# Rounding the head of h on VectorE, and fetching the scan's x operands two steps ahead

## The chip, the cores and the metric

The kernel runs on one core of a Trainium2 chip. The metric is device microseconds of one execution. The kernel before took 646.58, 649.59 and 651.04 us in three runs, median 649.59 us. The profile of it is of one further execution, of 646.94 us, whose span (first to last instruction) is 644.9 us.

## The reference, cut to what matters

Two layers. The first (fc1, a nearest-neighbour graph in 8x8 windows, an edge convolution with a maximum over neighbours, fc2, a residual) ends in an image x1 of 16 x 48 x 32 x 32. The second scans the rows of x1 with a ConvLSTM cell, once from the top and once from the bottom, and projects the hidden states of both:

```
def step(carry, xr):
    h, c = carry
    inp = jnp.concatenate([xr, h], axis=1)
    gates = lax.conv_general_dilated(inp, w_mid, (1,), 'SAME', dimension_numbers=dn) + b[None, :, None]
    i, f, g, o = jnp.split(gates, 4, axis=1)
    c2 = jax.nn.sigmoid(f) * c + jax.nn.sigmoid(i) * jnp.tanh(g)
    h2 = jax.nn.sigmoid(o) * jnp.tanh(c2)
    return ((h2, c2), h2)
hs_f = _convlstm_scan(xr, w_f[:, :, 1, :], b_f, reverse=False)
hs_b = _convlstm_scan(xr, w_b[:, :, 1, :], b_b, reverse=True)
feats = jnp.concatenate([hs_f, hs_b], axis=2)
feats = jnp.transpose(feats, (1, 2, 0, 3))
y = jnp.einsum('oc,bchw->bohw', w_proj, feats)
...
return jax.nn.relu(y) + x
```

## The kernel before, in words

The first layer is worked in 32 groups, called turns here; TensorE gathers neighbours with one-hot matmuls, ScalarE applies the GELU (`gel`), VectorE takes maxima (`hmax`, L1272), finds the next groups' neighbours (`idx`, L1248) and builds the one-hot operand (`onehot`, L1257). The neighbour indices go out to memory and come back spread over partitions: SP, whose queue issues nearly every transfer, stores `idx` (L326), waits until it has landed, and issues two spreads into `ib` (L335). Each turn SP also loads `xres` (L319), keys (L309) and `y_hl` (L300) and stores x1 rows (L345). The rows of x1 are split on the way into a rounded head and a rest and lie in `xh`, one slot a row. In turns 14 to 21 SP adds to each turn the weights of the scan (`wl_raw`, L404), small columns (`rests`, L420), a store of two finished rows to memory (`xl_d`, `store_lows`, L414) and a copy of two rows' twins within on-chip memory (`load_twins`, L426); rows 16 to 23 follow in turns 26 to 29 and rows 8 to 15 in scan steps 2 to 5.

The scan has 32 steps s of two directions d. For each, TensorE adds into two banks (`pz` or `p_edge`) an x part from `xt` (2 matmuls, L728), a top part from `xh` with the head of h (6 matmuls, L738), and a low part from `ht` (6 matmuls, L746: the rest of h, an unrounded copy of h, and a third of x). ScalarE takes tanh of the two banks (L926, L932), copies the other direction's h into `ht` (`h_edge`, L942), and takes tanh of the cell (L936). VectorE computes `cu` (L1370), `pz` (L1378), `c` (L1381) and `h` (L1388), in program order: cell of direction 0, `cu` of direction 1, cell of direction 1, `cu` of direction 0 of the next step. GpSimd (POOL) then rounds h into the slot of the next row in `xh` (`head`, L1155) and subtracts that head from h into `ht` (L1157). Each engine runs its own program in order; semaphores tie them. VectorE's steps 2 to 13 are a hardware loop, the others are written out.

SP in a scan step, for each direction: wait for the gates of this step, load the thirds of the next step into `ht` (a single buffer, L439), load the shifted x two steps ahead into `xt` (two buffers, L432), store h (`hist_d`, L493), load a residual row (`x1r`). From step 17 on it then loads two stored rows of h into `hp` (L503), after both directions. TensorE projects them (L757) one step later, between the x part and the top part of direction 0; from step 19 on ScalarE copies the projected row out (L947) and VectorE takes its statistics (`bst`, L1393).

Of the kernel before, what the change touches and what calls it, by code (L numbers as in the profile page):

```python
# [54 lines left out]
def build(nc, xs, xrow, w1, ones_sel, col1, jcol, wedge, edge_scale, edge_shift, ident9, w2, col2,  # L55
# [9 lines left out]
    with ExitStack() as ctx:  # L65
# [193 lines left out]
        @block.sync
        def _(sp):  # L260
# [180 lines left out]

            def turn(j, b):
                if isinstance(j, int) and nth(j, b, 0)[0] in (GROUPS - 4, GROUPS - 3):
# [3 lines left out]
                    sp.wait_ge(S["xl_stored0"], 32 * 8)  # L447
                    load_shifts(0, d)
                    load_thirds(0, d)
                    load_shifts(1, d)  # L450
# [4 lines left out]
                if isinstance(j, int) and j > 0:  # L455
                    at = nth(j, b, 0)[0] - (GROUPS - 18)
                    if at == 0:
                        sp.wait_ge(S["rests_set"], 1)
# [1058 lines left out]
```

## Time and profile before

| | us |
|---|---|
| median of 3 runs (lowest, highest) | 649.59 (646.58, 651.04) |
| the profiled execution, its span | 646.94, 644.9 |
| PE, DVE, ACT, POOL busy (share of span) | 549.8 (85%), 500.1 (78%), 437.1 (68%), 242.5 (38%) |
| first layer: first to last `hmax` | 76.1 to 348.8 |
| scan: first h to last h | 352.7 to 622.9 |

The busy shares are means over stages with different limits. In the first layer VectorE has work nearly all the time; in the scan no engine has, since each direction is a loop of dependent work and two such loops share the engines. An idle gap counts only where the work that ends last stands behind it.

### The profile page before, as it was taken

Reading aid. Unit: us, or ns where it says so; the run is one execution under the profiler, and the core shown is the slowest. Engines: PE = TensorE matmul, PEld = TensorE weight load, DVE = VectorE, ACT = ScalarE, POOL = GpSimd, SP = SyncE. Lnnn points to the kernel's source line nnn. Section 1 sums busy time; section 2 is a strip of 40 time slices with the busy share of each in tenths; the row PEclk is TensorE's granted clock in tenths of the full one; section 3 lists DMA queues with packets and bytes.
Section 4 is the critical chain, followed back from the end, with each engine's and each line's share of the span. In section 5 each row is a group of like instructions: output and inputs, shape, how many; then the busy total and the mean of one; then the engine's idle time right before and its main releaser. Section 6 shows DMA issues by size and latency. Waiting matters only on the chain.

```text
span 644.9 us, 11504 instructions
## 1 busy us (share of the span) xinstructions
PE 549.8 (85%) x3160; PEld 333.0 (52%) x3160; DVE 500.1 (78%) x963; ACT 437.1 (68%) x645; POOL 242.5 (38%) x299
## 2 busy tenths in 40 slices
PE   6983699999999978989868989999997988998860
PEld 1232466666665645656535555566664645555530
DVE  2587679999999998799988757777777466776765
ACT  4761379999999978689866655666665455565645
POOL 2740103333333332235834634444444233443310
PEclk9995589999999999799997999999999898999985
DMA  8847656656667877878653355444444444444416
GB/s 220 271 143 220 168 132 134 148 144 142 142 142 163 196 168 182 176 153 161 159 129 77 87 137 143 127 134 130 130 127 137 116 148 129 132 128 121 131 55 196
DMA packets 112517, 94.72 MB, mean 147 GB/s; under 512 B 54560, under 2 KB 86818, under 8 KB 112146
## 3 DMA queue, kind: packets, MB, share of 16 engines
q1 hardware_dynamic: 111714, 90.64, 55.3%
q10 hardware_dynamic: 768, 3.67, 2.2%
q8 instruction: 15, 0.25, 0.2%
q14 instruction: 20, 0.16, 0.1%
HBM read 65.61 MB, written 26.48 MB: 143 GB/s over the span
## 4 chain that ended last, share of the span: by engine, by line
DVE 31%; PE 19%; DMA 15%; issue 12%; SPq 12%; ACT 7%; POOL 2%; DVEq 1%; POOLq 0%; ACTq 0%
DVE hmax L1272 8%; DMA hp<-hist_d 5%; PE pz L738 4%; DVE onehot L1257 4%; DVE c L1381 3%; DVE cu L1370 3%; DMA idx_d<-idx 3%; PE pz L580 3%; DVE idx L1248 3%; PE p_edge L738 2%; DVE h L1388 2%; PE pz L746 2%; DMA x_d<-x1t 2%; SPq L426 2%; DVE pz L1378 2%
## 5 line engine op out<-in xcount | busy, mean ns | idle before, releaser
L1272 DVE TENSOR_REDUCE hmax<-gel 96x128 f32<-96x1024 f32 x128 | 151.9, 1204 | 11.0 <-ACT gel L871 10.9
L871 ACT ACTIVATE gel<-pz 96x1024 f32<-96x1024 f32 x128 | 130.5, 1020 | 31.7 <-PE pz L658 18.2
L1155 POOL CAST xh<-h 48x512 fp32r<-48x512 f32 x62 | 37.6, 606 | 145.3 <-DVE h L1388 143.1
L738 PE MATMUL pz<-xh,w_rows 128*112 128x512 f32 x258 | 72.2, 416 | 5.9 <-POOL xh L1155 5.7
L1157 POOL TENSOR_TENSOR ht<-h,xh 48x512 fp32r<-48x512 f32 x62 | 73.6, 1186 | 5.0
L746 PE MATMUL pz<-ht,w_rows 128*112 128x512 f32 x258 | 69.3, 404 | 3.7 <-DMA ht<-xl_d 3.7
L658 PE MATMUL pz<-onehot,ab_hi 64*96 64x512 f32 x256 | 60.4, 468 | 5.2 <-ACT gel L871 3.9
L738 PEld LDWEIGHTS pz<-xh,w_rows 128*112 128x112 f32 x258 | 43.2, 178 | 35.3 <-POOL xh L1155 17.3
L936 ACT ACTIVATE pz<-c 48x512 f32<-48x512 f32 x43 | 25.7, 599 | 50.2 <-DVE c L1381 50.2
L746 PEld LDWEIGHTS pz<-ht,w_rows 128*112 128x112 f32 x258 | 44.8, 177 | 22.6 <-DMA ht<-xl_d 7.6
L1257 DVE TENSOR_SCALAR onehot<-ib,jcol_sb 128x1024 fp32r<-128x1024 uint16 x64 | 48.1, 753 | 10.3 <-DMA ib<-idx_d 10.2
L1388 DVE SCALAR_TENSOR_TENSOR h<-tgo,pz 48x512 f32<-48x512 f32 x43 | 29.7, 690 | 30.6 <-ACT pz L936 29.4
L658 PE MATMUL pz<-ident,ab_lo 64*96 64x512 f32 x256 | 53.0, 408 | 0.0
L658 PE MATMUL pz<-ident,ab_hi 64*96 64x512 f32 x256 | 52.9, 407 | 0.0
L658 PE MATMUL pz<-onehot,ab_lo 64*96 64x512 f32 x256 | 52.8, 408 | 0.0
L1108 POOL TENSOR_TENSOR xh<-x1t,x1c 48x256 f32 (+1 forms) x32 | 32.4, 1012 | 49.4 <-DVE onehot L1257 48.8
L1094 POOL TENSOR_TENSOR x1t<-side,xres 112x256 f32<-112x256 f32 x32 | 24.1, 752 | 62.3 <-ACT side L878 42.4
L1370 DVE SCALAR_TENSOR_TENSOR cu<-pz,c 48x512 f32<-48x512 f32 x43 | 29.9, 695 | 18.3 <-ACT pz L926 17.5
L606 PE MATMUL p_keys<-kr,kl 128*64 128x64 f32 x512 | 23.2, 236 | 22.1 <-DVE idx L1248 11.1
L942 ACT ACTIVATE ht<-h 48x512 fp32r<-48x512 f32 x62 | 39.2, 632 | 1.5
L658 PEld LDWEIGHTS pz<-onehot,ab_hi 64*96 64x96 f32 x256 | 21.4, 162 | 33.1 <-issue 22.9
L738 PE MATMUL p_edge<-xh,w_rows 128*112 128x512 f32 x126 | 36.2, 424 | 2.3 <-POOL xh L1155 2.0
(147 smaller groups left out, 1136.3 us busy)
## 6 DMA issues: line engine op xcount, KB each, us to landing
ib<-idx_d SPq DMA_DIRECT2D x64, 256.0 KB, 4.4
xt<-xl_d SPq DMA_DIRECT2D x64, 197.6 KB
y_d<-y SPq DMA_DIRECT2D x32, 192.0 KB, 3.3
y_hl<-y_d SPq DMA_DIRECT2D x32, 192.0 KB, 4.0
hist_d<-h SPq DMA_DIRECT2D x62, 96.0 KB, 4.8
hp<-hist_d SPq DMA_DIRECT2D x30, 192.0 KB, 3.3
ht<-xl_d SPq DMA_DIRECT2D x128, 33.1 KB, 2.9
xl_d<-xh SPq DMA_DIRECT2D x16, 198.4 KB, 3.4
```

The lines of the kernel that those rows point to most:

```text
L658: mm = pe.matmul(pz[0:O, 2 * (t % 2) + s, :], part[rows, b, t, which], moving[rows], start=(n == 0), stop=(n == 3))
L738: pe.matmul(gate_banks(k, d)[m][0:TOP, :], w_rows[:, 0, d, m, t], by_column(row), start=False, stop=False)
L746: mm = pe.matmul(gate_banks(k, d)[m][0:TOP, :], w_rows[:, 1, d, m, t], by_column(ht[:, d, t:t + (W + 1) * B]), start=False, stop=(t == TAP ...
L871: act.activation(gel[:, t % 2], pz[0:O, 2 * (t % 2):2 * (t % 2) + 2, :], ACT.Gelu) \
L942: act.activation(h_slots(ht, HALF, d), h2[0:C, d].rearrange("p (b w) -> p b w", w=W), ACT.Copy) \
L1108: pool.tensor_tensor(slots(0, g)[:, 0], by_row(x1t[0:C, b]), by_row(x1c[0:C]).bitcast(F32), ALU.subtract).then_inc(S["x1_half"], 1)
L1155: pool.tensor_copy(head, columns(h2[0:C, d])).then_inc(S["h_top"], 1)
L1157: pool.tensor_tensor(h_slots(ht, 0, d), columns(h2[0:C, d]), head.bitcast(F32), ALU.subtract).then_inc(S["h_lo"], 1)
L1257: dve.tensor_scalar(onehot[:, b, 2 * half:2 * half + 2], ib[:, b, 2 * half:2 * half + 2], jcol_sb[:, 0:1], None, ALU.is_equal).then_inc(S[ ...
L1272: dve.tensor_reduce(dst, gel[:, t % 2].rearrange("p w (r c k) -> p w r c k", r=WS, k=KN), AX_X, ALU.max).then_inc(S["maxed"], 1)
L1370: dve.scalar_tensor_tensor(cu[HALF:TOP, d], gate_banks(k, d)[0][HALF:TOP, :], 1.0, c2[HALF:TOP, d], ALU.add, ALU.mult).then_inc(S["cells_k ...
L1388: dve.scalar_tensor_tensor(h2[0:C, d], tgo[HALF:TOP, d], 1.0, b_go[HALF:TOP, :], ALU.add, ALU.mult) \
```

## The change

1. VectorE rounds h into `xh` itself, right behind `h`, and with that takes over POOL's waits for the row stores. POOL only subtracts. VectorE's loop over steps 2 to 13 is written out.
2. `ht` has two buffers for each direction; the thirds are loaded two steps ahead, in the same place of SP's order.
3. The load of stored h moves from the end of SP's step to the middle, behind the store of direction 0.
4. Row stores and twin copies take four rows instead of two, and lie in turns 10, 11 and 18, 19 and 26, 27 (stores), 12, 13 and 20, 21 and 30, 31 (twins), and scan steps 2 and 3; weights go in turns 8 to 20, `rests` in 21 to 25. SP's program is written out from turn 8 on (from 14 before).

```diff
-        ht = sb("ht", [P, 2, SLOT], F32R)
+        ht = sb("ht", [P, 2, 2, SLOT], F32R)
...
-                sp.dma_start(xl_d[r:r + 2, first:first + rows].rearrange("r c n -> c r n"),
-                             xh[src:src + rows, r:r + 2, 0:SLOT - 1].bitcast(F32)).then_inc(S[sem], 16)
+                sp.dma_start(xl_d[r:r + 4, first:first + rows].rearrange("r c n -> c r n"),
+                             xh[src:src + rows, r:r + 4, 0:SLOT - 1].bitcast(F32)).then_inc(S[sem], 16)
...
-                    if at < 8:
-                        block, part = divmod(at, 4)
-                        sp.wait_ge(S["x1_split"], PAIRS * (block + 1))
-                        store_lows((0, 24)[block] + 2 * part, "xl_stored0")
-                        load_twins((0, 24)[block] + 2 * part, "x_twins0")
...
+                    if 8 <= g < 16:
+                        load_scan_weight(g - 8)
+                    elif 16 <= g < 21:
+                        load_tap_weight(g - 16)
+                    elif 21 <= g < 26:
+                        load_rest(g - 21)
+                    for first, r, n in ((10, 0, 0), (18, 24, 0), (26, 16, 1)):
+                        if first <= g < first + 2:
+                            sp.wait_ge(S["x1_split"], first - 2)
+                            store_lows(r + 4 * (g - first), f"xl_stored{n}")
+                        elif g in (first + 2, first + 3) and n == 0 or g >= 30 and n == 1:
+                            load_twins(r + 4 * (g % 2), f"x_twins{n}")
...
             def step(s):
                 for d in range(2):
-                    if s + 1 < H:
+                    if s + 2 < H:
                         sp.wait_ge(S["gates"], s * 4 + (2 * d + 2))
-                        load_thirds(s + 1, d)
-                    if s + 2 < H:
+                        load_thirds(s + 2, d)
                         load_shifts(s + 2, d)
                     store_h(s, d)
+                    if s >= H // 2 + 1 and d == 0:
+                        load_h(s - 1, 1 - s % 2)
                     if 6 <= s < H // 2 + 6:
                         load_x1r(s - 6, d)
-                    if 2 <= s < 6:
-                        (store_lows, load_twins)[d](4 + 2 * s, ("xl_stored1", "x_twins1")[d])
-                if s >= H // 2 + 1:
-                    load_h(s - 1, 1 - s % 2)
+                    if 2 <= s < 4:
+                        (store_lows, load_twins)[d](4 * s, ("xl_stored1", "x_twins1")[d])
...
-                pool.wait_ge(S["h2_ready"], s * 2 + (d + 1))
...
-                pool.tensor_copy(head, columns(h2[0:C, d])).then_inc(S["h_top"], 1)
                 pool.wait_ge(S["h_top"], s * 2 + (d + 1))
...
                 dve.scalar_tensor_tensor(h2[0:C, d], tgo[HALF:TOP, d], 1.0, b_go[HALF:TOP, :], ALU.add, ALU.mult) \
                     .then_inc(S["h2_ready"], 1)
+                if s + 1 < H:
+                    if s == 0:
+                        dve.wait_ge(S["xl_stored0"], 32 * 4)
+                    if s == 7 and d == 0:
+                        dve.wait_ge(S["xl_stored1"], 32 * 4)
+                    if s == H // 2 - 1 and d == 0:
+                        dve.wait_ge(S["gates"], 4 * (s + 1))
+                    dve.wait_ge(S["h2_ready"], s * 2 + (d + 1))
+                    dve.tensor_copy(head_slots(s + 1, d), h2[0:C, d].rearrange("p (b w) -> p b w", w=W)) \
+                        .then_inc(S["h_top"], 1)
...
-            with dve.Fori(0, 2) as j:
-                for k in range(2, 8):
-                    step(j * 6 + k, k)
-            for s in range(14, H):
+            for s in range(2, H):
```

VectorE in one scan step, from `c` of direction 0 on. Before:

```order
L1381 SCALAR_TENSOR_TENSOR c<-cu,pz 48x512 [waits cell_parts]
L1388 SCALAR_TENSOR_TENSOR h<-tgo,pz 48x512 [waits h_edge,h_lo,hist0,tanh_c]
L1370 SCALAR_TENSOR_TENSOR cu<-p_edge,c 48x512 [waits cells,tanh_if]
L1378 SCALAR_TENSOR_TENSOR p_edge<-p_edge,tgo 48x512 [waits cells_kept,tanh_go]
L1381 SCALAR_TENSOR_TENSOR c<-cu,p_edge 48x512 [waits cell_parts]
L1388 SCALAR_TENSOR_TENSOR h<-tgo,p_edge 48x512 [waits h_edge,h_lo,hist1,tanh_c]
```

Now:

```order
L1371 SCALAR_TENSOR_TENSOR c<-cu,pz 48x512 [waits cell_parts]
L1378 SCALAR_TENSOR_TENSOR h<-tgo,pz 48x512 [waits h_edge,h_lo,hist0,tanh_c]
L1388 CAST xh<-h 48x16x32 [waits h2_ready]
L1360 SCALAR_TENSOR_TENSOR cu<-pz,c 48x512 [waits cells,tanh_if]
L1368 SCALAR_TENSOR_TENSOR pz<-pz,tgo 48x512 [waits cells_kept,tanh_go]
L1371 SCALAR_TENSOR_TENSOR c<-cu,pz 48x512 [waits cell_parts]
L1378 SCALAR_TENSOR_TENSOR h<-tgo,pz 48x512 [waits h_edge,h_lo,hist1,tanh_c]
L1388 CAST xh<-h 48x16x32 [waits h2_ready]
```

One CAST stands between each `h` and the next `cu`, twice in a step; nothing else of VectorE's order in a step is changed (line numbers are those of each kernel's own text).

SP in a turn of the first layer, from the `ib` spreads to the next store of `idx`. Before (turns 14 to 18 have all four kinds of added transfers, 19 to 21 those without `rests`):

```order
L335 DMA ib<-idx_d 64x4x512 [waits onehots,idx_stored0]
L335 DMA ib<-idx_d 64x4x512
L404 DMA wl_raw<-wl 16x1344
L420 DMA rests<-ones_sel 16x1
L414 DMA xl_d<-xh 48x2x529 [waits x1_split]
L414 DMA xl_d<-xh 16x2x529
L426 DMA xh<-xh 16x2x529 x2
L319 DMA xres<-xrow 48x256 [waits x1_sum]
L319 DMA xres<-xrow 48x256
L326 DMA idx_d<-idx 128x4x8 [waits topk_done]
```

Now, the turns with the most (12 and 13):

```order
L339 DMA ib<-idx_d 64x4x512 [waits onehots,idx_stored1]
L339 DMA ib<-idx_d 64x4x512
L408 DMA wl_raw<-wl 48x1344
L430 DMA xh<-xh 16x4x529 x2
L323 DMA xres<-xrow 48x256 [waits x1_sum]
L323 DMA xres<-xrow 48x256
L330 DMA idx_d<-idx 128x4x8 [waits topk_done]
```

The store of rows is in other turns; the twin copies are one issue pair of twice the rows.

SP in a scan step after the 17th (`hist_d<-h` is the store of h, `ht<-xl_d` the thirds), from the store of direction 0 on. Before:

```order
L493 DMA hist_d<-h 48x512 [waits h2_ready]
L517 DMA x1r<-x_d 64x512
L439 DMA ht<-xl_d 16x529 [waits gates]
L439 DMA ht<-xl_d 16x529
L432 DMA xt<-xl_d 96x1x527
L493 DMA hist_d<-h 48x512 [waits h2_ready]
L511 DMA x1r<-x_d 48x512
L503 DMA hp<-hist_d 96x512 [waits hist0,hist1]
L503 DMA hp<-hist_d 96x512
```

Now:

```order
L492 DMA hist_d<-h 48x512 [waits h2_ready]
L502 DMA hp<-hist_d 96x512 [waits hist0,hist1]
L502 DMA hp<-hist_d 96x512
L516 DMA x1r<-x_d 64x512
L443 DMA ht<-xl_d 16x529 [waits gates]
L443 DMA ht<-xl_d 16x529
L436 DMA xt<-xl_d 96x1x527
L492 DMA hist_d<-h 48x512 [waits h2_ready]
L510 DMA x1r<-x_d 48x512
```

The load of `hp` stands in front of direction 1's thirds, shifts and store of h, instead of behind them.

## Rows read from the trace of the kernel before

**Rows 1.** VectorE in time (start us, us, what): `hmax` that ends a turn

```profile
214.27 0.69 DVE L1264 TENSOR_TENSOR hmax<-hmax,selfg 96x512 f32<-96x512 f32 x1
...
222.22 0.69 DVE L1264 TENSOR_TENSOR hmax<-hmax,selfg 96x512 f32<-96x512 f32 x1
...
295.58 0.69 DVE L1264 TENSOR_TENSOR hmax<-hmax,selfg 96x512 f32<-96x512 f32 x1
```

**Rows 2.** The same view, in brackets the idle time before: a late `ib`

```profile
333.17 0.75 DVE L1257 TENSOR_SCALAR onehot<-ib,jcol_sb 128x1024 fp32r<-128x1024 uint16 x1 [1.70 <-DMA ib<-idx_d]
```

**Rows 3.** SP's queue in time, an undisturbed turn

```profile
159.80 1.45 SPq L335 DMA_DIRECT2D ib<-idx_d  x2
...
162.11 0.85 SPq L319 DMA_DIRECT2D xres<-xrow  x2
...
164.35 0.43 SPq L326 DMA_DIRECT2D idx_d<-idx  x1
```

**Rows 4.** The same view, what a loaded turn adds: weights, row store, twins

```profile
248.35 0.60 SPq L404 DMA_DIRECT2D wl_raw<-wl  x1
...
249.00 0.90 SPq L414 DMA_DIRECT2D xl_d<-xh  x2
...
249.94 1.44 SPq L426 DMA_DIRECT2D xh<-xh  x2
```

**Rows 5.** VectorE in time, written-out scan: h, cu, next h

```profile
463.73 0.69 DVE L1388 SCALAR_TENSOR_TENSOR h<-tgo,pz 48x512 f32<-48x512 f32 x1 [0.67 <-ACT pz L936]
...
464.45 0.69 DVE L1370 SCALAR_TENSOR_TENSOR cu<-p_edge,c 48x512 f32<-48x512 f32 x1
...
467.34 0.69 DVE L1388 SCALAR_TENSOR_TENSOR h<-tgo,p_edge 48x512 f32<-48x512 f32 x1 [0.67 <-ACT p_edge L936]
```

**Rows 6.** VectorE in time, one-time work for the projection, step 17

```profile
483.81 1.12 DVE L1414 TENSOR_SCALAR wp_sb<-wp_sb 96x64 f32<-96x64 f32 x1
```

**Rows 7.** VectorE in time, hardware loop: h, direction 0, consecutive steps

```profile
448.70 0.69 DVE L1388 SCALAR_TENSOR_TENSOR h<-tgo,pz 48x512 f32<-48x512 f32 x1 [0.86 <-ACT pz L936]
...
456.31 0.69 DVE L1388 SCALAR_TENSOR_TENSOR h<-tgo,p_edge 48x512 f32<-48x512 f32 x1 [0.86 <-ACT p_edge L936]
```

**Rows 8.** Casts: VectorE's by source (ns min/median/max), POOL's on the page

```profile
L1195 DVE CAST y<-x_in x9: 427/489/647, 7.4 to 28.4; 128x512 fp32r<-128x512 f32 x9
...
L1155 POOL CAST xh<-h 48x512 fp32r<-48x512 f32 x62 | 37.6, 606 | 145.3 <-DVE h L1388 143.1
```

**Rows 9.** TensorE in time: two top parts in a row without a wait

```profile
520.86 1.67 PE L738 MATMUL pz<-xh,w_rows 128*112 128x512 f32 x6
...
524.26 1.59 PE L738 MATMUL pz<-xh,w_rows 128*112 128x512 f32 x6
```

**Rows 10.** VectorE in time: h of direction 0 in steps 0, 18 and 31

```profile
352.68 0.69 DVE L1388 SCALAR_TENSOR_TENSOR h<-tgo,pz 48x512 f32<-48x512 f32 x1 [0.66 <-ACT pz L936]
...
494.71 0.69 DVE L1388 SCALAR_TENSOR_TENSOR h<-tgo,pz 48x512 f32<-48x512 f32 x1 [0.66 <-ACT pz L936]
...
618.07 0.69 DVE L1388 SCALAR_TENSOR_TENSOR h<-tgo,p_edge 48x512 f32<-48x512 f32 x1 [0.66 <-ACT p_edge L936]
```

**Rows 11.** TensorE by lines, scan (busy, mean ns; idle before)

```profile
L746 PE MATMUL pz<-ht,w_rows 128*112 128x512 f32 x252 | 67.7, 404 | 3.7 <-DMA ht<-xl_d 3.7
...
L757 PE MATMUL p_keys<-hp,wp_sb 96*64 96x512 f32 x32 | 9.5, 676 | 10.3 <-DMA hp<-hist_d 10.3
```

**Rows 12.** VectorE in time with projection: h, cu, next step's h

```profile
547.66 0.69 DVE L1388 SCALAR_TENSOR_TENSOR h<-tgo,pz 48x512 f32<-48x512 f32 x1 [0.67 <-ACT pz L936]
...
548.88 0.69 DVE L1370 SCALAR_TENSOR_TENSOR cu<-p_edge,c 48x512 f32<-48x512 f32 x1 [0.53 <-ACT p_edge L926]
...
556.03 0.69 DVE L1388 SCALAR_TENSOR_TENSOR h<-tgo,pz 48x512 f32<-48x512 f32 x1 [0.67 <-ACT pz L936]
```

**Rows 13.** Busy us in 4 us (PE, PEld, DVE, ACT, POOL), PEclk, DMA

```profile
500.00:504.00 4.00, 4.00 (x12) 2.27 (x9) 0.00 (x0) 0.00 (x0) 0.93 (x1) 0.50 0.57 178
```

**Rows 14.** Transfers to or from `hist_d` in the scan

```profile
DMA to landing us min/median/max: 1.9/4.6/7.2
```

More of the change, by code:

```diff
@@ L249, in by_row, with h_slots, head_slots @@
             return t.rearrange("c (r w) -> c r w", w=W)
-        def h_slots(t, first, d):
-            return t[first:first + C, d, 1:1 + (W + 1) * B].rearrange("p (b w) -> p b w", w=W + 1)[:, :, 0:W]
+        def h_slots(first, d, b):
+            return ht[first:first + C, d, b, 1:1 + (W + 1) * B].rearrange("p (b w) -> p b w", w=W + 1)[:, :, 0:W]
         def row_of(s, d):
             return s if d == 0 else s * -1 + (H - 1)
+        def head_slots(s, d):
+            return xh[0:C, row_of(s, d), 1:1 + (W + 1) * B].rearrange("p (b w) -> p b w", w=W + 1)[:, :, 0:W]
         @block.sync
@@ L425, in load_twins @@
                 for first, src in ((C, HALF), (TOP, HALF + 16)):
-                    sp.dma_start(xh[first:first + 16, r:r + 2, 0:SLOT - 1].bitcast(F32),
-                                 xh[src:src + 16, r:r + 2, 0:SLOT - 1].bitcast(F32)).then_inc(S[sem], 16)
+                    sp.dma_start(xh[first:first + 16, r:r + 4, 0:SLOT - 1].bitcast(F32),
+                                 xh[src:src + 16, r:r + 4, 0:SLOT - 1].bitcast(F32)).then_inc(S[sem], 16)
             def load_shifts(s, d):
@@ L438, in load_thirds @@
                 for q in range(2):
-                    sp.dma_start(ht[HALF * q + C:HALF * q + HALF, d, 0:SLOT - 1].bitcast(F32),
-                                 xl_d[row_of(s, d), 32 + 16 * q:C + 16 * q]).then_inc(S[f"x_third{d}"], 16)
+                    sp.dma_start(ht[HALF * q + C:HALF * q + HALF, d, s % 2, 0:SLOT - 1].bitcast(F32),
+                                 xl_d[row_of(s, d), 32 + 16 * q:C + 16 * q]).then_inc(S[f"x_third{d}{s % 2}"], 16)
             def turn(j, b):
@@ L446, in turn @@
                     sp.wait_ge(S["pads_set"], 8)
[L447 to L450, printed above, removed]
+                    sp.wait_ge(S["xl_stored0"], 32 * 4)
+                    for s in range(2):
+                        load_shifts(s, d)
+                        load_thirds(s, d)
                 for k, stage in ((0, load_xres), (3, store_idx), (-2, store_x1), (5, load_keys), (4, load_y),
@@ L480, in _ @@
                 turn(0, b)
-            with sp.Fori(1, GROUPS // 2 - 9) as j:
+            with sp.Fori(1, 4) as j:
                 for b in range(2):
                     turn(j, b)
-            for j in range(GROUPS // 2 - 9, GROUPS // 2):
+            for j in range(4, GROUPS // 2):
                 for b in range(2):
@@ L540, in _ @@
                 step(s)
-            sp.wait_ge(S["xl_stored1"], 32 * 8)
+            sp.wait_ge(S["xl_stored1"], 32 * 4)
             for b in range(2):
@@ L739, in h_part @@
                                   start=False, stop=False)
-                pe.wait_ge(S[f"x_third{d}"], s * 32 + 32)
+                pe.wait_ge(S[f"x_third{d}{s % 2}"], s // 2 * 32 + 32)
                 if later(s):
@@ L774, in _ @@
             pe.wait_ge(S["first_rows"], 2)
-            pe.wait_ge(S["x_twins0"], 32 * 8)
+            pe.wait_ge(S["x_twins0"], 32 * 4)
             pe.wait_ge(S["wl_split"], 3)
@@ L787, in _ @@
                 step(s, s)
-            pe.wait_ge(S["x_twins1"], 32 * 8)
+            pe.wait_ge(S["x_twins1"], 32 * 4)
             for s in range(8, 14):
@@ L937, in tanh_cell, with h_edge @@
                     .then_inc(S["tanh_c"], 1)
-            def h_edge(s, d):
+            def h_edge(s, d, b):
                 act.wait_ge(S["h2_ready"], s * 2 + (d + 1))
-                act.activation(h_slots(ht, HALF, d), h2[0:C, d].rearrange("p (b w) -> p b w", w=W), ACT.Copy) \
+                act.activation(h_slots(HALF, d, b), h2[0:C, d].rearrange("p (b w) -> p b w", w=W), ACT.Copy) \
                     .then_inc(S["h_edge"], 1)
@@ L950, in step @@
                 for d in range(2):
[L951 removed]
+                    prev = (s - 1, 1, k % 2) if d == 0 else (s, 0, (k + 1) % 2)
                     more = later(s) if d == 0 else not isinstance(s, int) or s + 1 < H
@@ L1080, in first_rows @@
             def first_rows():
-                pool.wait_ge(S["xl_stored0"], 32 * 8)
+                pool.wait_ge(S["xl_stored0"], 32 * 4)
                 for n, row in enumerate((0, H - 1)):
@@ L1148, in columns @@
                     return t.rearrange("p (b w) -> p b w", w=W)
-                pool.wait_ge(S["h2_ready"], s * 2 + (d + 1))
-                if s == H // 2 - 1 and d == 0:
-                    pool.wait_ge(S["gates"], 4 * (s + 1))
-                head = xh[0:C, reg(row_of(s + 1, d), 0, 1), 1:1 + (W + 1) * B] \
-                    .rearrange("p o (b w) -> p (o b) w", w=W + 1)[:, :, 0:W]
-                pool.tensor_copy(head, columns(h2[0:C, d])).then_inc(S["h_top"], 1)
                 pool.wait_ge(S["h_top"], s * 2 + (d + 1))
-                pool.tensor_tensor(h_slots(ht, 0, d), columns(h2[0:C, d]), head.bitcast(F32),
+                pool.tensor_tensor(h_slots(0, d, (s + 1) % 2), columns(h2[0:C, d]), head_slots(s + 1, d).bitcast(F32),
                                    ALU.subtract).then_inc(S["h_lo"], 1)
```

23 lines of the change are left out of this document (4 added, 19 removed).

## The prediction, made before the changed kernel was run

> **What bounds the kernel now.** I read the chain of waits first, to see which engine is named in which stretch, then each engine's instructions in time in the three stretches that the change touches, then TensorE's groups with the idle time in front of them. In the first layer VectorE should be the bound: an undisturbed turn takes 222.22 - 214.27 = 7.95 us [rows 1]. The next eight turns, to 295.58, take 73.36 us where 8 x 7.95 = 63.6 would do, so 9.8 us are lost there; they are the turns whose `onehot` waits for a late `ib`, as it does once more at the end of the layer, for 1.70 us [rows 2]. What is late is SP. In an undisturbed turn SP has issued `ib` by 161.25 and can store the next `idx` at 164.35; of these 3.10 us `xres` takes 0.85, so 2.25 are free [rows 3]. A loaded turn adds 0.60 for weights, 0.90 for a row store and 1.44 for twins, 2.94 in all [rows 4]. SP falls back by 0.7 us or more a turn, and the `idx` store that it issues too late delays everything behind it.
>
> In the scan two loops of dependent work share the engines. TensorE needs 524.26 - 520.86 = 3.40 us for one direction's half-step, when nothing holds it [rows 9]. VectorE in the written-out steps needs 467.34 - 463.73 = 3.61 from h to h [rows 5]: `cu`, `pz`, `c`, 0.67 waiting for the tanh of the cell, h. Two halves are 7.22. In VectorE's hardware loop a step takes 456.31 - 448.70 = 7.61 [rows 7], since there h starts 0.86 rather than 0.67 behind the work before it. From step 0 to 18 the scan takes 494.71 - 352.68 = 142.0 us, 7.89 a step; from 18 to 31, with projection, 618.07 - 494.71 = 123.4 us, 9.49 a step [rows 10]. TensorE's idle time says what the difference to the smooth step is: 3.7 us before the low part, waiting for `ht`, and 10.3 us before half of the projections, waiting for `hp` [rows 11]. A step with projection that does not wait takes 556.03 - 547.66 = 8.37 [rows 12].
>
> **The change, part by part.** The sum is made against the profiled execution, 646.94 us; the median of the runs, 649.59, is 2.65 higher.
>
> *First layer.* The heaviest new turn has weights and the twins of four rows. If a copy of four rows costs SP what one of two rows did, that is 0.60 + 1.44 = 2.04, under the 2.25 that are free [rows 3, 4]; if it costs twice, 3.48, and SP falls back 1.2 us in each of two turns, twice, with unloaded turns behind them. The turns with row stores add 1.50. Gain at most 9.8, at least nothing (if `idx` lands as late as before); I take 8.0, since even the bad case loses in four turns rather than eight. At the end of the layer turns 28 and 29 lose their rows and twins and get two pairs of thirds: of the 1.70 [rows 2] I take 1.5. Together -9.5.
>
> *Scan, steps 0 to 18.* POOL's rounding (0.606) leaves the way from h to TensorE and a cast on VectorE comes in. The nearest row is VectorE's cast of 512 words, 0.427 at its shortest, 0.489 median, 0.647 at most, undisturbed at the low end [rows 8]. Its output there is contiguous; here it goes into 16 runs of 32 words, which no VectorE row shows. I take 0.43, with 0.03 to the next instruction as between h and `cu` (464.45 - 463.73 = 0.72 for an h of 0.69 [rows 5]): 0.46. TensorE gets the head about 0.2 us earlier, but VectorE works in order: `cu` of the other direction, and through it that direction's next h, now stand behind the cast. Half a step on VectorE becomes 3.61 + 0.46 = 4.07, a step 8.14. That is above TensorE's 6.80 and above the 7.61 of today, so VectorE alone sets the pace, and what waits for `ht` there was (3.7) or hardware loop (0.4 a step) is covered by it. 18 x 8.14 = 146.5, plus 1.1 of one-time work [rows 6], is 147.6 against 142.0: +5.6. This part costs time.
>
> *Scan, steps 18 to 31.* Projection adds VectorE's statistics and ScalarE's copy. In the unstalled step `cu` of direction 1 stands idle 0.53 behind ScalarE [rows 12]; the cast behind h of direction 0 fits into that. The other cast adds 0.46: 8.37 + 0.46 = 8.83, and 13 x 8.83 = 114.8 against 123.4, -8.6, if no projection waits. SP issues the load half a step, some 4 us, earlier, and TensorE's longest total here was 10.3 us over the projections of one bank. In front of the load SP now waits for h of the previous step to be stored: a transfer to or from `hist_d` takes 4.6 us at the median and 7.2 at most [rows 14], against about 4.4 between the two events, so SP is usually held little and at most some 2.8; behind it stand direction 1's thirds and shifts, due two steps later, and its store of h, due 4 us later. I take -8.0.
>
> *Doubled `ht`, four-row transfers in steps 2 and 3, the subtraction that starts earlier:* no price of their own, since TensorE's slack of 4.07 - 3.40 = 0.67 a half-step covers them; without it the 3.7 us of waits for `ht` [rows 11] would be what they can cost or give. *The tail* behind the last h is as before.
>
> Sum: 646.94 - 9.5 + 5.6 - 8.0 = 635.0.
>
> **Weighed against the Trainium skill.** The trace has the cast of 512 words at 0.427 us or more [rows 8]. The Trainium skill (VectorE: DVE Perf Modes, the section on the TRN2 errata) gives 58 cycles plus the elements over the mode's factor at 0.96 GHz: (58 + 256)/0.96, an estimate of 0.33 us. By the row the sum is 635.0; by the page each cast is 0.10 shorter, and the sum would be about 630. The row decides.
>
> **The rivals.**
>
> *The cast runs at one word a cycle, because of its runs of 32* (12 in 100). Nothing in the profile shows a fast VectorE write into such runs. Its price would be that of VectorE's other 512-word work, 0.69 [rows 5]: 0.26 more in 36 halves up to step 18 (9.5 us), in 13 halves of direction 1 (3.4), and 0.2 in direction 0's, where 0.53 was free (2.6): 650.5, slower than before. The gain is gone when the cast takes about 0.62, and beyond 0.73 the kernel is slower by over 1%. Against it speaks only that its source is one contiguous run. The same page of the Trainium skill (the section on what auto-detection checks) would have a single-source copy between SBUF tensors keep its doubled rate if the outer dimensions are even, which 16 is; no row of this case shows it.
>
> *SP stays late in the first layer* (13 in 100): four-row twins cost twice, and `idx` lands behind larger transfers. Then the 8.0 is missing: 643.0. Against it: only four turns carry twins, not eight.
>
> *`hp` stays late* (10 in 100): held by the wait for the stored h, the load starts no earlier than now, and each step with projection keeps 9.49 and gets the 0.46: 13 x 9.95 = 129.4, +6.0 in place of -8.0, 649.0.
>
> *TensorE's clock falls in the scan* (5 in 100). Behind one wait for `hp` the granted clock was 0.50, that is 1.2 GHz, from 500 to 504 us, with VectorE idle in all of it [rows 13]. TensorE will idle 16% of a step (6.80 of 8.14). At half the clock its half-step is 6.8, a step 13.6 and 5.5 too long: two such steps eat the gain, four make it slower by 1%; six, 668. Against it: the drop stood behind a long wait, and what idles now is 0.67 at a time.
>
> **How the numbers follow.** The forecast, with VectorE as the scan's bound and SP on time, gets 60 in 100 and gives 635; since the profiled execution is the low end of three runs that spread 0.7%, I say 636 for the median. About 1% is what a measurement here can tell from no change. Best case: 9.8 and 1.7 in the first layer, 8.6 in the scan: 632.4, less the 3.0 by which the lowest run lies under its median: 629. The upper end takes in late SP and late `hp` and reaches 650, at the edge of the slow cast. Faster by over 1% means under 643.1: the forecast's 60, half of late SP (7), and 1 of late `hp`: 0.68. Slower by over 1%, above 656.1: 5 of the slow cast and 3 of the clock, 0.08. The rest, 0.24, within 1%.
>
> **What would show it.** Right: `hmax` rows 7.95 apart from 222 to 296 with no `onehot` behind `ib`; a cast of 0.43 between each h and `cu`; h of one direction 8.1 apart up to step 18 and 8.8 after it, with `cu` no longer idle behind ScalarE; no wait for `ht` and next to none for `hp`; no PEclk at 0.5 in the scan. Wrong: a cast near 0.7; steps still at 7.6, which would mean that VectorE is not held; `ib` waits in the turns with twins; `hp` waits of over 1 us.

## The result, and the profile after

Over 20 runs each the changed kernel takes 642.07 us at the median, the kernel before 646.91; the ratio is 0.9933, 95% interval 0.9905 to 0.996. (The ratio is not quite that of the medians, since it leaves out the few runs that fell into a slower state.) It is faster by 0.7%, where 2% was forecast. The profiled execution took 645.08 us, 3.0 above its median, with a span of 643.3 us.

VectorE in time (start us, us, line, operation, idle time before in brackets and what ended it) answers to [rows 1]. Up to the first row shown the turns are 7.95 us apart, as forecast, the last of them 8.25; then come two bad ones, of 9.60 and 11.97 us:

```profile
198.81 0.69 DVE L1254 TENSOR_TENSOR hmax<-hmax,selfg 96x512 f32<-96x512 f32 x1
...
202.19 0.75 DVE L1247 TENSOR_SCALAR onehot<-ib,jcol_sb 128x1024 fp32r<-128x1024 uint16 x1 [1.56 <-DMA ib<-idx_d]
...
208.41 1.08 DVE L1254 TENSOR_TENSOR hmax<-hmax,selfg 96x512 f32<-96x512 f32 x1
...
220.38 0.69 DVE L1254 TENSOR_TENSOR hmax<-hmax,selfg 96x512 f32<-96x512 f32 x1
...
332.54 0.75 DVE L1247 TENSOR_SCALAR onehot<-ib,jcol_sb 128x1024 fp32r<-128x1024 uint16 x1 [3.28 <-DMA ib<-idx_d]
```

Two more turns, to 277.31 and 286.15, take 9.18 and 8.84. Over turns 1 to 25 that is 8.2 us above 7.95 a turn; the kernel before lost 10.2 by the same count. The last row answers to [rows 2]: the wait at the layer's end is 3.28 us, not gone, as forecast, but twice as long.

SP's queue in time, behind rows 4 to 7's store and ahead of the bad turns, answers to [rows 3, 4]:

```profile
181.15 2.83 SPq L323 DMA_DIRECT2D xres<-xrow  x2
...
188.82 1.34 SPq L430 DMA_DIRECT2D xh<-xh  x2
190.21 1.31 SPq L323 DMA_DIRECT2D xres<-xrow  x2
191.56 0.43 SPq L330 DMA_DIRECT2D idx_d<-idx  x1
...
196.94 1.33 SPq L339 DMA_DIRECT2D ib<-idx_d  x2
```

The copy of four rows' twins costs SP 1.34 us, no more than that of two (1.44). Two things are late. Behind a four-row store the issue of `xres` takes 2.83 us in place of 0.85 (3.34 a turn before), so SP itself falls back. And the landing is late: `idx` was stored at 191.56, and SP, which waits for it, could issue `ib` only at 196.94. The windows of the same stretch (busy us of PE, PEld, DVE, ACT, POOL; PEclk; share of the DMA engines; GB/s) show how much the DMA engines carry then:

```profile
190.00:198.00 8.00, 6.94 (x54) 4.33 (x50) 7.69 (x20) 7.07 (x11) 1.30 (x3) 1.00 0.99 174
198.00:206.00 8.00, 7.54 (x66) 4.88 (x66) 6.33 (x19) 6.57 (x10) 2.72 (x4) 1.00 0.95 143
206.00:214.00 8.00, 5.68 (x40) 4.28 (x42) 6.56 (x11) 4.75 (x7) 2.52 (x4) 0.75 0.96 186
```

The DMA engines are 95 to 99% busy; in undisturbed turns, from 110 to 142 us, the share is 0.60 to 0.62. The share is no exact measure: a short window can come out above 1 (1.28 below). And the clock falls: TensorE's keys come late (first row below), it does nothing from 206 to 208 us, and from 210 to 216 its granted clock is half, 1.2 GHz (second row). In the turn of 11.97 no `onehot` waits for `ib`; the late keys and the half clock make it. The layer's end has the same: 0.50 from 334 to 342 us, behind the 3.28 us wait.

```profile
208.32 0.69 PE L604 MATMUL p_keys<-kr,kl 128*64 128x64 f32 x16 [2.58 <-DMA kr<-xn_d]
```

```profile
212.00:214.00 2.00, 2.00 (x10) 1.83 (x12) 2.00 (x6) 1.83 (x3) 0.73 (x1) 0.50 1.28 150
```

This is not new in the change. In the kernel before, in the turn of 11.60 us within the 73.36 of [rows 1], the keys come 1.71 us late and the granted clock is 0.50 from 260 to 266 us:

```profile
258.32 0.69 PE L606 MATMUL p_keys<-kr,kl 128*64 128x64 f32 x16 [1.71 <-DMA kr<-xn_d]
```

```profile
262.00:264.00 2.00, 2.00 (x12) 1.83 (x10) 1.33 (x6) 1.87 (x3) 0.11 (x1) 0.50 0.99 219
```

In the scan the steady rhythm is the one forecast. VectorE from h to h, to be held against [rows 5]:

```profile
455.45 0.69 DVE L1378 SCALAR_TENSOR_TENSOR h<-tgo,pz 48x512 f32<-48x512 f32 x1 [0.66 <-ACT pz L934]
456.17 0.42 DVE L1388 CAST xh<-h 48x512 fp32r<-48x512 f32 x1
456.62 0.69 DVE L1360 SCALAR_TENSOR_TENSOR cu<-p_edge,c 48x512 f32<-48x512 f32 x1
...
459.51 0.69 DVE L1378 SCALAR_TENSOR_TENSOR h<-tgo,p_edge 48x512 f32<-48x512 f32 x1 [0.66 <-ACT p_edge L934]
```

Half a step is 4.06. By its source line (ns min/median/max) the cast answers to [rows 8], at the price that was taken:

```profile
L1388 DVE CAST xh<-h x62: 418/419/421, 351.2 to 612.0; 48x512 fp32r<-48x512 f32 x62
```

Steps 0, 18 and 31 of direction 0, the counterpart of [rows 10], and two waits in steps 3 and 4:

```profile
350.42 0.69 DVE L1378 SCALAR_TENSOR_TENSOR h<-tgo,pz 48x512 f32<-48x512 f32 x1 [0.66 <-ACT pz L934]
...
381.07 0.69 DVE L1378 SCALAR_TENSOR_TENSOR h<-tgo,pz 48x512 f32<-48x512 f32 x1 [2.46 <-DMA hist_d<-h]
...
390.43 0.69 DVE L1378 SCALAR_TENSOR_TENSOR h<-tgo,pz 48x512 f32<-48x512 f32 x1 [1.53 <-DMA hist_d<-h]
...
500.95 0.69 DVE L1378 SCALAR_TENSOR_TENSOR h<-tgo,pz 48x512 f32<-48x512 f32 x1 [0.66 <-ACT pz L934]
...
615.96 0.69 DVE L1378 SCALAR_TENSOR_TENSOR h<-tgo,p_edge 48x512 f32<-48x512 f32 x1 [0.66 <-ACT p_edge L934]
```

Step 0 to 18 takes 150.53 us (before 142.03), 18 to 31 takes 115.01 (before 123.36). TensorE by lines, against [rows 11], says who waits for whom now: the waits for `hp` are down from 10.3 us to 1.7, those for `ht` from 3.7 to nothing, and TensorE's top parts stand idle for 17.2 us, 16.5 of them behind VectorE's cast.

```profile
L736 PE MATMUL pz<-xh,w_rows 128*112 128x512 f32 x246 | 68.7, 414 | 17.2 <-DVE xh L1388 16.5
L744 PE MATMUL pz<-ht,w_rows 128*112 128x512 f32 x250 | 66.2, 400 | 0.0
...
L755 PE MATMUL p_keys<-hp,wp_sb 96*64 96x512 f32 x32 | 8.6, 618 | 1.7 <-DMA hp<-hist_d 1.6
```

### The profile page after: what moved, and what is told of

Its sections match the earlier page's. It is cut to its first block, busy times and chain, and to the rows that moved or that the text cites. A ratio compares the mean times of both kernels' runs of the same rounds, so it can differ in the third digit from the quotient of the medians.

```text
span 643.3 us, 11294 instructions
## 1 busy us (share of the span) xinstructions
PE 549.3 (85%) x3160; PEld 330.5 (51%) x3160; DVE 525.1 (82%) x1025; ACT 436.7 (68%) x645; POOL 209.1 (33%) x237
## 4 chain that ended last, share of the span: by engine, by line
DVE 41%; DMA 18%; SPq 15%; issue 14%; ACT 6%; PE 4%; DVEq 1%; ACTq 0%; POOL 0%; POOLq 0%
DVE hmax L1262 7%; DMA hist_d<-h 6%; DVE cu L1360 5%; DVE c L1371 5%; DMA idx_d<-idx 5%; DVE h L1378 4%; DVE pz L1368 4%; DVE onehot L1247 3%; DMA y_d<-y 3%; SPq L323 3%; ACT pz L934 2%; DVE idx L1238 2%; SPq L443 2%; SPq L339 2%; DMA ib<-idx_d 2%
## 5 line engine op out<-in xcount | busy, mean ns | idle before, releaser
L736 PE MATMUL pz<-xh,w_rows 128*112 128x512 f32 x258 | 71.9, 414 | 17.2 <-DVE xh L1388 16.5
L744 PEld LDWEIGHTS pz<-ht,w_rows 128*112 128x112 f32 x258 | 45.0, 175 | 16.5 <-issue 0.7
L617 PE MATMUL p_edge<-we_hi,y_hl 97*128 97x192 f32 x128 | 34.0, 301 | 5.0 <-DMA y_hl<-y_d 4.3
L934 ACT ACTIVATE p_edge<-c 48x512 f32<-48x512 f32 x21 | 12.5, 597 | 35.2 <-DVE c L1371 35.2
```

The lines of the kernel that those rows point to most:

```text
L617: pe.matmul(o, lhs, we_hi[0:O + 1, 0:2].rearrange("p a o -> p (a o)"), start=(t % 2 == 0), stop=False, skip_group_check=True)
L736: pe.matmul(gate_banks(k, d)[m][0:TOP, :], w_rows[:, 0, d, m, t], by_column(row), start=False, stop=False)
L744: mm = pe.matmul(gate_banks(k, d)[m][0:TOP, :], w_rows[:, 1, d, m, t], by_column(ht[:, d, s % 2, t:t + (W + 1) * B]), start=False, stop=(t ...
L934: act.activation(gate_banks(k, d)[1][HALF:TOP, :], c2[HALF:TOP, d], ACT.Tanh, scale=0.5) \
```

## The experiments

All ratios are to the kernel before, run on the same chip in the same batch, with 95% intervals.

**The parts by themselves.** The load of stored h alone, in the kernel before:

```
                     store_h(s, d)
+                    if s >= H // 2 + 1 and d == 0:
+                        load_h(s - 1, 1 - s % 2)
...
-                if s >= H // 2 + 1:
-                    load_h(s - 1, 1 - s % 2)
```

> The kernel before with one part alone: the load of stored h in the middle of SP's step. Theory (late hp was the whole excess behind step 18): the waits for hp fall from 10.3 us to under 1, steps behind 18 from 9.49 to about 8.6, some 10 us less: 636 to 640 us. Rival (it needs the doubled ht or the cast's place too, or SP is held by the wait for the stored row): waits for hp stay above 5 us, 643 us or more.

Measured: 0.9842 (0.9797 to 0.9887), 10.2 us of 646.9. TensorE's longest total of waits for `hp` falls from 10.3 us to 0.4. The two moved lines alone give more than twice what the whole change gives; neither the second `ht` buffer nor the cast is needed for it.

The cast alone, in the kernel before (VectorE's loop written out, POOL only subtracts):

```
-                pool.tensor_copy(head, columns(h2[0:C, d])).then_inc(S["h_top"], 1)
...
+                    dve.wait_ge(S["h2_ready"], s * 2 + (d + 1))
+                    dve.tensor_copy(head_slots(s + 1, d), h2[0:C, d].rearrange("p (b w) -> p b w", w=W)) \
+                        .then_inc(S["h_top"], 1)
```

> The kernel before with one part alone: VectorE rounds h, its loop written out. Theory (the cast costs a half-step 0.45 us): steps up to 18 go from 7.89 to 8.1 or more (4 to 8 us longer), behind 18 the waits for hp stay and the cast adds to some of it (0 to 6 us longer): 651 to 661 us. Rival (the shorter way from h to TensorE pays, and the written-out loop 0.4 a step): 640 to 646 us.

Measured: 1.0116 (1.0066 to 1.0167), 7.5 us slower. The steady step is 8.12 us, and without the earlier load TensorE still waits for `hp`:

```profile
L761 PE MATMUL p_keys<-hp,wp_sb 96*64 96x512 f32 x32 | 9.3, 660 | 11.2 <-DMA hp<-hist_d 11.0
```

The changed kernel without its first part, everything else kept: the cast goes back to POOL, with POOL's waits.

```
-                    dve.tensor_copy(head_slots(s + 1, d), h2[0:C, d].rearrange("p (b w) -> p b w", w=W)) \
-                        .then_inc(S["h_top"], 1)
...
+                pool.wait_ge(S["h2_ready"], s * 2 + (d + 1))
+                pool.tensor_copy(head_slots(s + 1, d), columns(h2[0:C, d])).then_inc(S["h_top"], 1)
```

> The changed kernel with the rounding of h put back on POOL, all else as changed. Theory (VectorE's cast sets the pace of the scan, 4.06 us a half-step): without the cast a half-step falls to VectorE's own 3.61 or little more, steps up to 18 to 7.3 from 8.12, steps behind 18 to about 8.4 from 8.82, that is 14 us and 5 us less: about 623 to 628 us, below both kernels. Rival (the doubled buffers and the earlier thirds give nothing, and POOL's 0.61 us of rounding stands on the way to TensorE again): steps up to 18 go back to about 7.9, behind 18 stay at 8.8: about 638 us.

Measured: 0.9719 (0.9677 to 0.9761), so 13.8 us below the change. VectorE in time:

```profile
349.87 0.69 DVE L1384 SCALAR_TENSOR_TENSOR h<-tgo,pz 48x512 f32<-48x512 f32 x1 [0.66 <-ACT pz L934]
...
459.87 0.69 DVE L1384 SCALAR_TENSOR_TENSOR h<-tgo,pz 48x512 f32<-48x512 f32 x1 [0.66 <-ACT pz L934]
...
463.48 0.69 DVE L1384 SCALAR_TENSOR_TENSOR h<-tgo,p_edge 48x512 f32<-48x512 f32 x1 [0.66 <-ACT p_edge L934]
...
490.77 0.69 DVE L1384 SCALAR_TENSOR_TENSOR h<-tgo,pz 48x512 f32<-48x512 f32 x1 [0.66 <-ACT pz L934]
...
600.68 0.69 DVE L1384 SCALAR_TENSOR_TENSOR h<-tgo,p_edge 48x512 f32<-48x512 f32 x1 [0.66 <-ACT p_edge L934]
```

Half a step is 3.61 again, a step 7.36, and 8.37 with projection; steps 0 to 18 take 140.90 us, 18 to 31 take 109.91, together 14.7 less than in the change. The theory holds for the rhythm: VectorE's cast sets the scan's pace in the change. The gain is under the 19 us that were expected, since steps 1 to 4 lose 6.7 us over the rhythm here and 3.3 in the change. POOL's rounding is slower (0.60 us), yet TensorE's top parts into `pz` stand idle for 8.8 us in all where they do so for 17.2 with VectorE's. The second `ht` buffer and the written-out loop were not run alone; what this kernel gains beyond the moved load and the first layer (18.2 - 10.2 - 2.3, an estimate of 5.7 us) is theirs together, with an uncertainty nearly as large.

**The first layer.** The changed kernel with the first layer's transfers as before:

```
-                    for first, r, n in ((10, 0, 0), (18, 24, 0), (26, 16, 1)):
...
+                    if at < 8:
+                        block, part = divmod(at, 4)
+                        sp.wait_ge(S["x1_split"], PAIRS * (block + 1))
+                        store_lows((0, 24)[block] + 2 * part, "xl_stored0")
+                        load_twins((0, 24)[block] + 2 * part, "x_twins0")
```

> The changed kernel with the first layer's transfers put back as in the kernel before (two-row stores and twins and a weight in each of turns 14 to 21, rows 16 to 23 in turns 26 to 29); scan as changed. Theory (the four-row pieces only moved the full stretch, they gave some 2 us): about 2 us slower than the change, ratio 0.995 to 0.999, and turns 17 to 24 lose 9 to 11 us. Rival (as forecast: they gave 8 to 9.5 us, and the profile of the change was unlucky): ratio 1.005 or more.

Measured: 0.9969 (0.9936 to 1.0002), against 0.9933 for the change. So the new spread gives about 0.4% (2.3 us), not sure to be more than nothing since the intervals overlap; the forecast had 9.5. In the profiles turns 1 to 25 lose 7.6 us in this kernel, less than the 9 to 11 expected, and 8.2 in the change. Profiles of one and the same first layer differ by as much: as before it lost 10.2, 11.5 and 7.6 us (the kernel before, the cast alone, this one), as changed 8.2, 6.5 and 10.4 (the change, the kernel with the cast on POOL, and the one with POOL's queue below).

The copies of rows 0 to 7 with 8 columns in place of 529, the count of transfers unchanged:

```
+                n = SLOT - 1 if r >= 8 else 8
...
-                                 xh[src:src + 16, r:r + 4, 0:SLOT - 1].bitcast(F32)).then_inc(S[sem], 16)
+                                 xh[src:src + 16, r:r + 4, 0:n].bitcast(F32)).then_inc(S[sem], 16)
```

> The changed kernel, with the twin copies of rows 0 to 7 (turns 12 and 13) cut from 529 columns to 8, the same count of transfers; the rest of their columns is filled once, ahead of turn 2, with other data, so its output differs there. The twins of rows 24 to 31 (turns 20 and 21) stay whole. Theory (the twins' traffic makes the idx store land late): the turns that end at 208.4 and 220.4 us and take 9.6 and 11.97 us fall to 7.95, 5.7 us less, and no wait for ib stands there, while the waits behind turns 20 and 21 stay: about 637 us, plus up to 3 for the fill. Rival (SP's time to issue makes it late): both stay as they are, 642 us or more.

Measured: 0.9875 (0.9833 to 0.9917); the interval just overlaps that of the change. VectorE in time:

```profile
192.83 0.69 DVE L1264 TENSOR_TENSOR hmax<-hmax,selfg 96x512 f32<-96x512 f32 x1
...
202.69 0.69 DVE L1264 TENSOR_TENSOR hmax<-hmax,selfg 96x512 f32<-96x512 f32 x1
...
210.64 0.69 DVE L1264 TENSOR_TENSOR hmax<-hmax,selfg 96x512 f32<-96x512 f32 x1
```

One turn of 9.86 us stays, now the first behind the row stores of turns 10 and 11; the next seven are 7.95 to 7.97 again, the one of 11.97 among them. Turns 1 to 25 lose 3.4 us, not 8.2; 3.9 of the difference are in the turns of the thinned copies. SP issues as many transfers as before and takes as long (1.35 and 1.30 us for the copies, 2.99 and 2.58 for `xres` behind the row stores), so for these turns it is the copies' traffic that costs, not SP's time to issue them. The row stores, which this kernel leaves whole, are followed by the turn that stays, which the theory had not said.

The weights out of these turns, on the kernel with the cast on POOL (SP's first turns are written out for it):

```
+                    if 2 <= g < 10:
+                        load_scan_weight(g - 2)
+                    if 4 <= g < 9:
+                        load_tap_weight(g - 4)
```

> On the kernel with the cast on POOL (e1_pool_cast, 0.972 of before): the 13 weight loads leave turns 8 to 20 and go into turns 2 to 9, the 5 small columns into turns 14 to 17 and 22; rows and twins stay in four-row pieces where the change put them. Theory (the DMA engines are full in turns 10 to 13 and 18 to 21, where rows or twins and weights meet, so that idx lands late): with 84 to 252 KB less in each of these turns the waits for ib shrink, and of the 6 to 8 us lost over turns 12 to 24 at least 4 come back: ratio 0.963 to 0.967. Rival (the four-row pieces alone hold the idx store behind them): the loss stays, ratio 0.970 to 0.973.

Measured: 0.9655 (0.9603 to 0.9707), in the range of the theory but with an interval that overlaps that of the base, 0.9719. The profile speaks against the theory: turns 1 to 25 lose 7.4 us, in the base 6.5, so the 4 us did not come back. Of the two blocks of bad turns the second is gone (turns 18 to 25 lose 0.1 us), but the first loses 7.2, with `onehot` behind `ib` in four turns, as the rival has it. That the weights matter is not shown; why only one block profits stays open.

Then everything spread evenly, two rows at a time, one kind of transfer a turn:

```
+                        if first <= g < first + 4:
+                            sp.wait_ge(S["x1_split"], first - 2)
+                            store_lows(r + 2 * (g - first), f"xl_stored{n}")
+                        elif first + 4 <= g < first + 8 and n == 0:
+                            load_twins(r + 2 * (g - first - 4), f"x_twins{n}")
...
-                    if 2 <= s < 4:
-                        (store_lows, load_twins)[d](4 * s, ("xl_stored1", "x_twins1")[d])
+                    if 2 <= s < 6:
+                        (store_lows, load_twins)[d](4 + 2 * s, ("xl_stored1", "x_twins1")[d])
```

> As e5_weights_early, and rows and twins in two-row pieces, one kind a turn: rows in turns 10 to 13, 18 to 21, 26 to 29, twins in turns 14 to 17, 22 to 25, and rows 8 to 15 over scan steps 2 to 5, as in the kernel before. Theory (full DMA engines): no turn from 2 to 25 takes over 8.2 us, the 6 to 8 us are gone, and scan steps 2 to 5 lose some 2 us less than with four-row pieces: ratio 0.956 to 0.962. Rival (one idx store in the same queue behind any row store is late, however small): turns behind row stores still take 9 us, ratio 0.966 or more.

Measured: 0.9517 (0.9475 to 0.9559), 619.74 us at the median in its batch: with its variant below the fastest, and 31 us below the kernel before. Turns 1 to 25 lose 0.7 us. The same spread on the changed kernel, cast kept on VectorE (beside the lines above, the pieces):

```
-                    sp.dma_start(xl_d[r:r + 4, first:first + rows].rearrange("r c n -> c r n"),
-                                 xh[src:src + rows, r:r + 4, 0:SLOT - 1].bitcast(F32)).then_inc(S[sem], 16)
+                    sp.dma_start(xl_d[r:r + 2, first:first + rows].rearrange("r c n -> c r n"),
+                                 xh[src:src + rows, r:r + 2, 0:SLOT - 1].bitcast(F32)).then_inc(S[sem], 16)
```

> The changed kernel, cast on VectorE kept, with the even spread of e6_even_spread: weights in turns 2 to 9, rows and twins in two-row pieces, one kind a turn, and in scan steps 2 to 5. Theory (the whole gap between forecast and result is full DMA engines in turns 12 to 24 and in scan steps 2 to 4): no turn from 2 to 25 over 8.2 us, some 7 us less there, and some 2 less in steps 1 to 5 (full steps of 8.12 remain): ratio to before 0.978 to 0.982, 633 to 635 us where before takes 647. Rival (with VectorE's cast the scan does not keep the gain, or the first layer's end gives it back): 0.988 or more.

Measured: 0.9737 (0.9693 to 0.9782), a little better than expected. Its windows (columns as above), and VectorE in time, h of steps 0, 18 and 31:

```profile
190.00:198.00 8.00, 7.67 (x75) 4.86 (x72) 7.89 (x20) 7.30 (x11) 2.88 (x4) 1.00 0.75 175
198.00:206.00 8.00, 7.69 (x76) 4.89 (x70) 7.89 (x20) 7.30 (x11) 3.09 (x4) 1.00 0.67 165
206.00:214.00 8.00, 7.68 (x74) 4.88 (x70) 7.89 (x20) 7.30 (x11) 2.88 (x4) 1.00 0.75 161
```

```profile
340.48 0.69 DVE L1378 SCALAR_TENSOR_TENSOR h<-tgo,pz 48x512 f32<-48x512 f32 x1 [0.66 <-ACT pz L934]
...
488.42 0.69 DVE L1378 SCALAR_TENSOR_TENSOR h<-tgo,pz 48x512 f32<-48x512 f32 x1 [0.66 <-ACT pz L934]
...
602.38 0.69 DVE L1378 SCALAR_TENSOR_TENSOR h<-tgo,p_edge 48x512 f32<-48x512 f32 x1 [0.66 <-ACT p_edge L934]
```

The throughput is nearly the same (161 to 175 GB/s, in the change 143 to 186), but the engines are 67 to 75% busy, VectorE 7.89 of 8 us, and the clock stays full. The share of the engines alone does not tell which turns lose, though. In the kernel with the thin copies a stretch with a share above 1 loses nothing:

```profile
206.00:214.00 8.00, 7.73 (x70) 4.88 (x66) 7.89 (x20) 7.51 (x11) 2.92 (x5) 1.00 1.03 206
```

The lossy turns of the kernel before, from 222 to 286 us, have shares of 0.72 to 0.91, and the even spread on POOL's cast has 0.68 to 0.83 there without a loss. What is shown is that this spread, smaller pieces with the weights out of their way, takes the loss away in three profiles (0.2 us here, 0.7 on POOL's cast, 0.2 in the variant below); since moving the weights alone left most of it, the pieces are needed. Whether they help through SP's issues or through the landing was not separated. Turns 1 to 25 lose 0.2 us here, step 0 starts 9.9 us earlier than in the change, and steps 0 to 18 take 147.94: the forecast's 147.6. With it the forecast's 635 would have been reached: 0.9737 of 646.9 is 629.9. Of the 5 us beyond, 2.7 are in the first layer, since step 0 starts at 340.48 where the forecast has 352.68 - 9.5 = 343.2: the last six turns take 49.5 us, before 53.3, more than the forecast's 1.5.

**Steps 3 and 4 of the scan.** Rows 8 to 15 issued by POOL, on its own queue:

```
+                    if 2 <= s < 4:
+                        (store_lows, load_twins)[d](4 * s, ("xl_stored2", "x_twins2")[d])
...
+                    pool.dma_start(xl_d[r:r + 4, first:first + rows].rearrange("r c n -> c r n"),
```

> On e1_pool_cast: in scan steps 2 and 3 the row stores and twin copies of rows 8 to 15 are issued by POOL on its own queue and no longer by SP. Theory (SP's queue is the obstacle: the thirds and the store of h wait 3 us behind a four-row store that was issued first): SP's issues of ht take 0.9 us again, no h waits for the store of h, steps 1 to 4 lose under 2 us where they lost 6.7, so about 5 us less: ratio 0.963 to 0.966. Rival (the DMA engines are the obstacle, whichever queue feeds them, or POOL's own issuing delays its casts): steps 2 to 4 stay above 9 us, ratio 0.970 or more.

Measured: 0.9643 (0.9595 to 0.969), which the theory would have, but its rows contradict the theory:

```profile
372.75 0.88 SPq L443 DMA_DIRECT2D ht<-xl_d  x2
...
375.51 1.31 SPq L443 DMA_DIRECT2D ht<-xl_d  x2
```

```profile
383.77 0.69 DVE L1400 SCALAR_TENSOR_TENSOR h<-tgo,pz 48x512 f32<-48x512 f32 x1 [3.12 <-DMA hist_d<-h]
```

SP issues in 0.9 to 1.4 us where it took 3.0, yet h still waits for its store, 7.1 us in all (9.2 with SP's queue), and steps 3 and 4 take 10.57 and 8.62 us (10.43 and 9.15); TensorE's granted clock, 0.61 from 386 to 390 us here and full in the base, may add to them. So SP's issuing is at most a small part of it. What both queues share are the DMA engines, busy 0.87 and 0.75 of the time from 376 to 384 us; that they are the obstacle is what is left, not shown by itself. The Trainium skill (DMA: Bandwidth & Descriptors, the section on issuing engines not being separate queues) says that transfers issued by SP, ACT and POOL run on the same 16 engines and interleave; the 3.12 us wait agrees. The rival's rows are not all there either: of steps 2 to 4 only one stays above 9 us. The better ratio has little counterpart in these steps and none elsewhere in this profile, whose first layer loses 10.4 us (6.5 in the base); its interval overlaps that of the base. With two-row pieces (e6) steps 1 to 4 lose 2.5 us where four-row pieces lose 6.7.

The last try moves rows 12 to 15 from steps 4 and 5 to 6 and 7:

```
-                    if 2 <= s < 6:
+                    if s in (2, 3, 6, 7):
```

> On e6_even_spread (0.952 of before): the two-row pieces of rows 12 to 15 go from scan steps 4 and 5 to steps 6 and 7, with their waits. Theory (x1's last rows, the first stores of h and these pieces meet in steps 2 to 5): steps 2 to 5 lose about 1 us less, steps 6 and 7 nothing: ratio 0.949 to 0.951. Rival (two-row pieces no longer cost anything there, what is left has another cause): same as e6, 0.951 to 0.953.

Measured: 0.9521 (0.9474 to 0.9568), the same as e6: a miss. Steps 2 to 5 take 31.35 us, in e6 31.39, so nothing was gained there. Steps 7 and 8 now take 8.82 and 9.35 us, in e6 7.50 and 7.38; there h waits 1.97 and 2.06 us for its store in direction 0, where e6 has waits of 0.83 to 1.13 around these steps:

```profile
404.90 0.69 DVE L1391 SCALAR_TENSOR_TENSOR h<-tgo,pz 48x512 f32<-48x512 f32 x1 [1.97 <-DMA hist_d<-h]
...
414.25 0.69 DVE L1391 SCALAR_TENSOR_TENSOR h<-tgo,pz 48x512 f32<-48x512 f32 x1 [2.06 <-DMA hist_d<-h]
```

## Why the prediction was right in direction and wrong in size

- **First layer, -9.5: this step failed.** Measured -2.3 (h of step 0 at 350.42, before 352.68), which is not clear of noise. The term that failed is the 8.0, taken "since even the bad case loses in four turns rather than eight": it priced twins and stores by their own issues on SP and let `idx` land as ever. SP's price for the twins was right, four rows cost no more than two. Left out was that behind a four-row store SP's next issue takes 2.83 to 3.34 us in place of 0.85, and that `idx` and `kr` land late, while the DMA engines are 95 to 99% busy; twice TensorE's long idle behind that was followed by 6 to 8 us at half clock. With the thin copies 3.4 of the 8.2 us are left, with the even spread 0.2. That the DMA engines are the reason is argued, not shown. Its rival of late SP, at 643.0, names nearly the right time and half of the mechanism (`idx` landing behind larger transfers); part of that is luck, since it took -2.4 for the scan where the profile has +0.2.
- **The loss before was read too simply.** The prediction put the 9.8 us of [rows 1] down to SP alone. 3.65 of them are the turn of 11.60 us, in which keys that landed late and the half clock stand beside a wait for `ib` (2.04 us).
- **Scan, steps 0 to 18, +5.6.** Measured +8.5. The cast (0.43 taken, 0.419 measured) and the step (8.14, measured 8.12) are right, so the price for one word a cycle falls, and so does the 0.33 that the Trainium skill's row for VectorE gives (VectorE: DVE Perf Modes, the section on the TRN2 errata); the same section says that this row comes out too low. Mis-sized is what was costed at nothing, "four-row transfers in steps 2 and 3": in the change h waits for its own store, and steps 3 and 4 take 10.29 and 8.99, 3.0 us over the rhythm. With two-row pieces and the even spread these steps take 8.49 and 8.13.
- **Scan, steps 18 to 31, -8.0.** Measured -8.35. `cu` no longer stands idle, steps settle at 8.82 (forecast 8.83), and no clock drop is left, where the kernel before had one from 500 to 504 us [rows 13]. SP's new wait for stored h holds it 17.3 us in 11 times, 2.9 at most (2.8 forecast); in the same steps h waits four times for its store (0.74 to 1.21 us), and steps 19 to 22 together take 1.1 us more than four of 8.82. With the even spread h does not wait there, and this part comes to -9.4.
- **Tail.** +0.5 (27.34 against 26.83 us behind the last direction-0 h), forecast 0.
- **The sum** in the profiles is -2.3 + 8.5 - 8.35 + 0.5 = -1.6 us of span, by medians -4.8; the forecast had -11.9. The missing 7 to 10 us are the first layer and steps 0 to 18. By the parts run alone: -10.2 for the load, +7.5 for the cast, about -2.3 for the first layer, together -5.0, near the -4.3 that 0.9933 means. That this fits is in part luck, since the parts do not add: the cast costs more in the change than alone, and the second buffer and the loop, worth an estimated 5.7 us without it, are in no part of this sum.
- **What it did not ask** is what the scan would be without the cast. It compared 8.14 with the 7.89 of before, but the rest of the change lowers the step to 7.36, so the cast costs 14 us (0.9737 against 0.9517 with the spread, 0.9933 against 0.9719 without), twice what it costs alone.

## What to carry to other kernels

A large transfer must be priced by what lands behind it too, not only by what its own issue costs: look at the next issues on the same queue and at the small transfer that everybody waits for, and try smaller pieces spread over more turns. Here that spread was worth 13 us with either cast (0.9933 to 0.9737, 0.9719 to 0.9517). A copy taken from an idle engine to the engine that sets the pace costs its length every time (0.45 us in a half-step of 3.61), and more once other waits that hid it are gone. Where a change has several parts, run each alone: here one part of two lines was worth more than the whole.

## What was not expected of the hardware

One late transfer was paid twice. The keys came 2.58 us late, and TensorE then ran at a granted clock of 0.50 to 0.51 from 210 to 216 us, so that a turn took 11.97 us; the kernel before has the same once, with 1.71 us and 11.60. A step that was written out for VectorE cost some 0.25 us less than one of its hardware loop, for the same operations (7.36 against 7.61 us; in the kernel before the written-out steps 14 and 15 have 7.33 and 7.58). No run changed the loop alone. VectorE's cast into 16 runs of 32 words took 0.419 us, where its two-operand work of as many words takes 0.69.
